# Layer 3 attention on Trainium2: the causal mask of a corner as one full-height product in place of eight products in row strips

## The reference, cut to what matters

```python
def _L3_attn_ref(x, Wq, bq, Wk, bk, Wv, bv, Wo, bo):     # 16 heads of 8; sequences of 256 tokens
    q, k, v = heads(x @ Wq.T + bq), heads(x @ Wk.T + bk), heads(x @ Wv.T + bv)
    scores = einsum('bhqd,bhkd->bhqk', q, k) / sqrt(8)
    scores = scores + where(q_pos >= k_pos, -slope[h] * abs(q_pos - k_pos), -inf)
    attn = softmax(scores, axis=-1)
    return einsum('bhqk,bhkd->bhqd', attn, v) @ Wo.T + bo
```

## Time and profile before

| | |
|---|---|
| median of 3 runs | 2474.96 us |
| lowest and highest run | 2468.89 and 2475.29 us |
| the profiled execution | 2463.91 us |
| its span | 2462.2 us |
| mean granted TensorE clock in it | 0.894 of full speed |

### The profile page before, as it was taken

How to read it: one execution, slowest core, us unless ns; L and a number is a source line. 1 busy time by engine, 2 the same in 40 slices (tenths; PEclk the granted TensorE clock), 3 DMA queues, 4 the chain that set the end, 5 groups by cost and what they waited for, 6 DMA issues and landing times. The chain is left out here.

```text
span 2462.2 us, 41326 instructions
## 1 busy us (share of the span) xinstructions
PE 2040.5 (83%) x14039; PEld 1319.4 (54%) x14039; DVE 1458.4 (59%) x4086; ACT 1179.5 (48%) x2380; POOL 443.8 (18%) x522
## 2 busy tenths in 40 slices
PE   3435998468759999999999999999796188989978
PEld 3223996347744555555555555555596034444447
DVE  4675223642166777777777777777464766666615
ACT  1122553234436666666666666666232205555563
POOL 0154551044410111111110000000065100000000
PEclk9866998768959999999999999999898558898899
DMA  3412662045460000000000000001175322322101
GB/s 128 130 41 92 230 228 81 9 136 179 153 172 20 10 10 10 10 10 10 10 6 1 1 1 1 1 1 53 61 254 175 102 71 83 104 66 76 51 4 35
DMA packets 120234, 173.06 MB, mean 70 GB/s; under 512 B 16136, under 2 KB 79344, under 8 KB 119584
## 3 DMA queue, kind: packets, MB, share of 16 engines
q1 hardware_dynamic: 108016, 141.38, 18.2%
q0 software_dynamic: 11584, 23.91, 2.8%
q10 hardware_dynamic: 432, 5.19, 0.5%
HBM read 68.27 MB, written 45.40 MB: 46 GB/s over the span
## 5 line engine op out<-in xcount | busy, mean ns | idle before, releaser
L1797 ACT ACTIVATE t_p<-t_p,t_low 128x512 f32<-128x512 f32 x512 | 369.3, 721 | 333.4 <-DVE t_low L1868 333.3
L1868 DVE CUSTOM_DVE_ANT_0 t_p<-bank,L_skewed 128x512 f32<-128x512 f32 x512 | 332.6, 687 | 276.8 <-PE bank L1690 276.8
L129 PE MATMUL pair<-ident,t_p 128*128 128x128 f32 x2048 | 279.9, 280 | 0.0
L129 PEld LDWEIGHTS pair<-ident,t_p 128*128 128x128 f32 x2048 | 219.0, 141 | 94.8 <-issue 92.6
L2205 ACT ACTIVATE alibi_p<-pair 128x1024 f32<-128x1024 f32 (+1 forms) x192 | 169.0, 884 | 164.6 <-PE pair L2092 164.4
L2264 DVE CUSTOM_DVE_ANT_0 alibi_junk<-bank,alibi_later 128x512 bf16<-128x512 f32 (+1 forms) x256 | 150.8, 623 | 95.2 <-PE bank L2104 92.8
L1947 POOL COPY t_wide<-t_inverse 128x512 f32<-128x512 f32 x64 | 39.1, 611 | 892.2 <-DVE t_inverse L1884 883.4
L2104 PE MATMUL bank<-alibi_k_aug,alibi_q_aug 32*128 32x512 f32 (+1 forms) x256 | 105.3, 559 | 36.7 <-DMA alibi_k_aug<-aug_k 16.8
L1690 PEld LDWEIGHTS bank<-t_k_hi,t_q_hi 64*128 64x128 f32 x512 | 47.7, 183 | 161.6 <-issue 149.6
L1690 PE MATMUL bank<-t_k_hi,t_q_hi 64*128 64x512 f32 x512 | 127.8, 496 | 3.5 <-DVE t_low L1868 3.2
L1712 PE MATMUL pair<-t_pT,t_v 128*64 128x512 f32 x512 | 123.8, 605 | 1.6 <-DVE t_hT L1891 1.6
(11 more groups left out here) (488 smaller groups left out, 4401.6 us busy)
## 6 DMA issues: line engine op xcount, KB each, us to landing
L0moe_w<-L_packed SPq DMA_DIRECT2D x39, 578.0 KB, 3.4
L2moe_w<-L_skewed SPq DMA_DIRECT2D x39, 450.0 KB, 3.1
L1moe_w<-L_packed SPq DMA_DIRECT2D x23, 578.0 KB, 3.4
alibi_q_aug<-aug_q SPq DMA_DIRECT2D x8, 1024.0 KB, 7.6
alibi_k_aug<-aug_k SPq DMA_DIRECT2D x8, 1024.0 KB, 8.1
L_skewed<-bias_table SPq DMA_DIRECT2D x16, 448.0 KB, 10.3
slots<-g ACTq DMA_DIRECT2D x3, 1690.0 KB, 11.9
L0moe_xs<-slots SPq DMA_DIRECT2D x39, 130.0 KB, 3.2
```

The costliest lines, as they stand in the source:

```text
L129: last = nc.tensor.transpose(out[0:piece.shape[1], j * P:j * P + piece.shape[0]], piece, ident[0:piece.shape[0], 0:piece.shape[0]])
L1797: nc.scalar.activation(p[:, u % RING, :], p[:, u % RING, :], ACT.Exp, bias=low[:, u % 16:u % 16 + 1], scale=-1.0, accum_out=sums[:, n % 2, ...
L1868: nc.vector.tensor_tensor_reduce(out=p[:, u % RING, :], in0=score_ps[h][:], in1=skewed[:, (n % PAIRS) * 2 + h, start:start + SEQ], scale=- ...
```

## The change

The eight products in the row strips become, for each head of the half, one product over all 128 rows: `k.before` as weights, `hide` as the moving operand. For `quad` 1 one product covers both corners of a head, 256 columns in all, through a view that takes the first and the last 128 columns of the bank. So a tick has two mask products, each with 128 or 256 columns. The tiles `one` and `veil` go, with the POOL instructions that laid them (two memsets, eight `affine_select`s) and their semaphores; the first mask waits for `hide_laid` in place of `veiled`.

```diff
-        one, veil = st.sb("one", [P, 4, P], BF16), st.sb("veil", [P, 4, P], BF16)
...
-            def veils(n, j):
-                u = n * TICKS + j
-                quad, half = j % 6 // 2, j % 2
+            def veil(n, j):
+                u, quad = n * TICKS + j, j % 6 // 2
                 if u == 0:
-                    pe.wait_ge(veiled, 8)
-                for part in range(4):
-                    w = 32 * (part + 1)
-                    for c, a, e in regions(quad):
-                        for r in (2 * half, 2 * half + 1):
-                            ins = nc.tensor.matmul(flip_ps[u % 2][:, r % 2, a:a + w], one[rows(r), part, :], veil[rows(r), part, 0:w],
-                                                   start=False, stop=True, skip_group_check=True)
+                    pe.wait_ge(hide_laid, 1)
+                for half in range(2):
+                    bank = flip_ps[u % 2][:, half, :].rearrange("p (c n) -> p c n", n=P)
+                    corners = bank[:, 0:TPS:3, :] if quad == 1 else bank[:, 0:1, :]
+                    ins = nc.tensor.matmul(corners, k.before[:], hide[:].unsqueeze(1).to_broadcast([P, corners.shape[1], P]),
+                                           start=False, stop=True, skip_group_check=True)
                 ins.then_inc(flipped, 1)
...
-            nc.gpsimd.memset(one[:], 0.0).then_inc(cleared, 1)
-            nc.gpsimd.memset(veil[:], 0.0).then_inc(cleared, 1)
-            pool.wait_ge(cleared, 2)
-            for r in range(4):
-                nc.gpsimd.affine_select(out=one[rows(r)], in_=one[rows(r)], compare_op=ALU.not_equal, fill=1.0, base=0,
-                                        pattern=[[-32, 4], [1, P]], channel_multiplier=-1).then_inc(veiled, 1)
-                nc.gpsimd.affine_select(out=veil[rows(r)], in_=veil[rows(r)], compare_op=ALU.is_ge, fill=LOWEST, base=0,
-                                        pattern=[[-32, 4], [1, P]], channel_multiplier=-1).then_inc(veiled, 1)
-            pool.wait_ge(veiled, 8)
```

More of the change, by code:

```diff
@@ L2041, in alibi_attention_block @@
         ones_cleared, ones_laid, hide_laid, later_laid = (st.sem(n) for n in ("ones_cleared", "ones_laid", "hide_laid", "later_laid"))
-        cleared, veiled = st.sem("cleared"), st.sem("veiled")
         odd_made, odd_taken = st.sem("odd_made"), st.sem("odd_taken")
@@ L2188, in _ @@
                     if 0 <= n < NB:
-                        veils(n, j)
+                        veil(n, j)
                     if j % 2 == 1 and j >= 3 and 0 <= n < NB:
```

## The result

| | median | lowest | highest | runs |
|---|---|---|---|---|
| before | 2469.01 us | 2466.43 | 2479.53 | 14 |
| after | 2484.70 us | 2478.45 | 2500.11 | 14 |

A forecast was written before the change was run, and what follows sets the result against it. PE was taken as the longest member of a ring with ACT and DVE. 2.1 us for each of seven batches, 0.3 for the last and one for half clock gave +16 us, 2475 to 2491; range 2470 to 2505.

The forecast's parts named there:

- Emptying: On PE, a product using another cut of the array starts 0.07 us before the modelled end of all in it.
- Duration of the masks: In each tick, the two full-height mask products last 0.285 us, or 0.39 us with two corners.
- Mix ticks pay, job ticks do not: Per batch, ticks with the mix behind the mask cost 2.3 us; the eight with an odd job sum to about 0.
- Cover in ticks 16 to 22: Next flips start about 0.3 us later, hidden by the score product's wait for DVE; costed at nothing, uncovered +10 us.
- A batch: Each of seven batches with scores beside it takes 2.1 us more, the last 0.3 us more.
- The ring takes it up: Rival: delays fall mainly into PE's waits for DVE and ACT, a third of the cost, +5 us, 2480; chance 0.14.
- Issue: Rival: PE's pace is that of its instructions, so 208 fewer products a batch pay, giving 2384 us; chance 0.05.
- POOL's operands: Removed POOL work, eight selects of 0.63 us and two memsets, is hidden by 60 us of other work; worth nothing.
- Signs: Expected in the profile after: high-clock batch 45.8 us for 43.7, DVE's score waits up about 2 us a batch, as many spells.
- The clock: Rival: the stage's 1.2 GHz spells, 4.3 us each, vanish (2466 us) or grow by two (2500); chance they go 0.14.

The follow-up runs named there:

- e5: Before with full-height masks only in the odd ticks and strip masks kept in the even ones; 2493.39 us, ratio to before 1.011.
- e6: Before with full-height masks only in the even ticks and strip masks kept in the odd ones; 2458.28 us, ratio to before 0.997.
- e7: After without any mask product on the transposed scores, the exponential taken of a thousandth of the score; 2448.99 us, ratio to before 0.993.
- e4: After with each full-height mask product issued twice; 2468.94 us, ratio to before 0.999.
- e2: After with the full-height mask moved first in each tick, ahead of the flips, which add to it; 2445.14 us, ratio to before 0.990.
- e9: Before with two idle full-height products of 512 columns in each of the 24 ticks before the first flips; 2478.52 us, ratio to before 1.003.
- e1: After with the full-height mask moved between flips and scores of its tick; median 2609.58 us, six runs from 2556.94 to 2692.13.

## Why the prediction was right

The forecast was 2491 us from a median of 2475. Before came out at 2469.0 us in the larger set and after at 2484.7, so the difference, +15.7 us, is the forecast +16. The steps held in the main, but several single sizes were off and made up for one another, so that the agreement within 1 us is partly luck. Point by point:

- *Emptying.* The array takes a product of another cut only 0.07 us before the end of what is in it. Shown in after by the mask behind the late score product (2168.28 against 2168.35); the 35.0 us of unnamed waits at the mask's loads fit it. The Trainium skill, TensorEngine Tiling (Array Packing), "Key Properties", says that changing the tiling mode drains TensorE. The trace agrees, with these two times.
- *Duration of the masks.* Forecast 0.285 and 0.39 us a pair; measured 0.28 and 0.39.
- *Mix ticks pay, job ticks do not.* Forecast about 16 us and about 0; e5 and e6 give 14 and 3 at one clock, and ticks 2 to 15 of one batch +1.69 and -0.33 us. Starts forecast at 0.215, 0.32, 0.11 and 0.21 behind the mask; measured 0.22, 0.32, 0.13 and 0.23. No drain between mask and turn. Off were single ticks. A mix tick in which the flips end last was put at +0.045 us, with strip masks that had ended 0.17 us behind. In tick 5, which has no late score product, they had ended 0.05 us behind (2088.84 + 0.33 = 2089.17, the scores 2088.62 + 0.50 = 2089.12), and it pays 0.21. Tick 9 pays nothing, as its mix waits for ACT in both (0.50 and 0.48 us). The job ticks that gain do so by up to 0.16 us, not 0.06 to 0.09.
- *Cover in ticks 16 to 22.* Flips of tick 17 later by 0.3 us, and the scores behind them wait for DVE on, 0.36 us in place of 0.67. Ticks 18 and 20 are covered likewise by the table of twenty ticks; tick 22 was not compared at one clock.
- *A batch* +2.1 us at one clock: measured +2.7 us between batches at 0.92 and 0.93, and 2.3 us by the twenty ticks at 2.4 GHz. The step is right, its size a tenth to a fourth too small; in whole runs it is +17 at one clock for the forecast +15. The last batch cost 0.8 us, not 0.3.
- *The ring takes it up*: fell as a whole, since the time rose by more than its 5 us. In part it is so: PE's waits for ACT and DVE shrank by 2 and 10 us, more than the 1.6 us that the sum took off for the ring, and about the 10 us that it put under cover in ticks 16 to 22.
- *Issue*: fell, by e7 above all. 2048 products gone gave 10 ns each. The 62 ns for each product without hardware decode that the Trainium skill names (TensorE: Matmul & The Clock Gate, "Wait — 56ns, not 53.3ns?") do not bind here; which decode mode is on, no run shows.
- *POOL's operands*: costed at nothing; not tried by itself, and no run parts them from the masks.
- *Signs.* The batch at high clock at 45.8 us can't be looked for: no batch of after with scores beside it lies above 0.93 as a whole; 43.7 us and the 2.3 of the twenty ticks would be 46.0. DVE's waits went up by 3 us a batch for the 2 put. The spells at 1.2 GHz after the start were to be as many as before; the profile of after has seven in place of five, most of them shorter, 78 us together in place of 82, and the start at 1.2 GHz is 41 us longer.
- *The clock* was held to be a toss-up between two sides. By the median of the runs nothing moved, 0.891 and 0.891. That I had named idle pieces at the end of a batch as what decides, at 4.3 us a spell, is not borne out: e4 has twice the mask products of after and a clock 0.10 higher over 320 us, and no run moved an idle piece alone. In other arrangements this term reached 25 us and more, larger than the change itself, and my range of 35 us owes its hit to its not having moved; that is luck. What in an instruction stream the clock follows stays open: with more full-height products than before it was higher in e2, e4 and e6, the same in after and lower in e5, and idle ones of 512 columns did not hold it in e9.

## What to carry to other kernels

A product that uses all rows of TensorE among products in row strips starts only when the array is all but empty (0.07 us before the end here), and so does the strip product behind it; it also loses the cover of whatever strip product was late. Its own columns are no small part: here 0.12 of 0.22 us with 128 columns a product, 0.22 of 0.32 us with 256. If it must be, put it where the array is empty anyway: behind other full-height work, or at the head of a group, where it may open the bank. Read every difference of a per cent beside the granted clock of its runs, and compare at like clock, before an explanation by work is believed.

## What the runs showed that I had not expected

- Issuing 384 products more made the changed kernel faster, 2484.7 to 2468.9 us, at a clock of 0.909 in place of 0.891.
- In one execution of e1 the stage stayed at 1.2 GHz for 534 us with PE counted as busy for 510 of them.
- At the same products and shapes, the mask's place within a tick moved the time from 2445 us (e2, first) over 2485 (after, last) to between 2557 and 2692 us (e1, between flips and scores).
- The granted clock of one kernel differs between executions, 0.882 to 0.896 in 59 of before, and most of their scatter of 29 us goes with it: a line in the time at 1.2 GHz leaves all of them within 6 us.
